# Linear attention stage: scores in row groups of 32, values in column groups by head pair, squares summed with the mask stationary

## The chip, the cores and the metric

One Trainium2 chip, one of its cores. The metric is the device time of one launch in microseconds (us), lower is better. The core has TensorE (PE: matmuls; PEld is its weight load), VectorE (DVE), ScalarE (ACT), GpSimd (POOL) and SyncE (SP, which issues the DMAs). Each engine works through its own instruction list in order, and waits for the others by semaphores.

## The reference

The kernel computes five residual layers on x (32 sequences of 32 tokens, 256 features). Only one of them, `L1_attn`, is touched. It works on chunks of 16 tokens with a carried matrix W; since the score mask and the carried state together are linear, the kernel computes it as causal attention without softmax over each sequence:

```python
q = l2norm(silu(short_conv(h @ Wq.T, conv_q)).reshape(b, l, 16, 16))   # k likewise, v without l2norm
inter = einsum('bqhk,bhkv->bqhv', q_c, W)            # W starts as W_init
qk    = einsum('bqhd,bkhd->bhqk', q_c, k_c) * tril
intra = einsum('bhqk,bkhv->bqhv', qk, v_c)
W_new = W + einsum('bchk,bchv->bhkv', k_c, v_c)
o = layernorm_per_head(inter + intra) * ln_gamma + ln_beta
out = (o * (h @ Wg.T)) @ Wo.T
```

There are 16 heads of 16 features, so 8 heads lie on 128 partitions, and everything is fp32.

## The kernel before

The program is six stages (cross attention, a selective scan, attention with experts, an alignment by dynamic programming, this linear attention, and a last expert layer), each written as one function per engine: `t_load`, `t_pe`, `t_act`, `t_dve`, `t_pool` here. There is no scheduler: the order of the Python lines is the order on each engine, and every wait is written out. Activations lie with features on partitions, as two groups c of 128, and 1024 tokens along the free axis, in 8 tiles t of 128 tokens (4 sequences each).

The stage in order:

1. Layer norm (`norm_pe`, `norm_act`, `norm_dve`). Then `dense_pe` (L201) makes 16 groups of 128x512: q, k, v and the gate (n = 0 to 3). ACT copies each to SBUF (L2025).
2. DVE runs the short convolution of q, k, v, six halves in a row, four instructions each (L2077, L2080). ACT applies Silu in place (L2030) and squares q and k (L2034); it does so only after all 16 copies.
3. PE sums the squares of each head (L1948): 32 matmuls in which a 128x128 block of squares is the stationary operand and the head mask (8 columns) streams. ACT takes the root (L2037), DVE the reciprocal (L2087) and spreads it over the 16 features (L2088). PE turns v (L1957) and the spread norms (L1967), DVE multiplies q and k by them (L2093, eight instructions).
4. The tile loop. POOL builds q times the head mask, so that eight heads stand side by side (L2160, two of 128x1024 a tile). `sc(t)` multiplies k by it (L1978, four matmuls of 512 columns into PSUM banks 0 to 3), DVE masks the four banks (L2100), and PE adds, in bank 4 or 5, q times W_init (L1989) and for each head its scores (128x128, stationary) times 16 columns of v (L1994), 16 matmuls a tile. ACT evicts the tile (L2047).
5. The per-head layer norm in two halves (`centre`, `variance`, `scaled`), the turn back (L2002), the gate (L2136), the output projection (L2010) and the residual add (L2152). `centre(0)` stands in the tile loop ahead of the last mask, `variance(0)` and `scaled(0)` behind it. The next stage starts at the small MEMSET on L174.

An fp32 matmul shows in the trace as two records, each with a weight load of its own; a transpose as one.

Of the kernel before, what the change touches and what calls it, by code (L numbers as in the profile page):

```python
# [13 lines left out]
ALU = mybir.AluOpType  # L14
# [50 lines left out]
         + [(3, "tile_qblk", "d_ms", TT), (3, "tile_norm", "d_tm", TT), (3, "tile_rec", "d_add", TT)]  # L65
# [64 lines left out]
def build(nc, A, out, first=0, last=5):  # L130
    ctx = ExitStack()
    with ctx:
# [1784 lines left out]
        t_qm = [view(26 * K + 2048 * j, DC, HPC, P) for j in range(2)]  # L1917
        t_S = [view(30 * K + 2048 * j, XH, P) for j in range(2)]
# [5 lines left out]
        t_ns = view(38 * K, 2, 2 * P)  # L1924
# [11 lines left out]
        def t_pe(pe):  # L1936
            norm_pe(pe, "tn", xT, U[2])
            pe.wait_ge(*S.at("tn_out", 2))
            pe.wait_ge(*S.at("ld_t", dma_n["ld_t"]))
            dense_pe(pe, "tp", [(P, [(t_w[n][:, k, m * P:(m + 1) * P], half(U[1], k, h)) for k in range(DC)])  # L1940
                                for n in range(4) for m in range(DC) for h in range(NH)], "a" * 16, list(range(8)))

            pe.wait_ge(*S.at("tp_ev_a", 16))
# [6 lines left out]
            mm.then_inc(S["t_ss"], 1)  # L1950
            pe.wait_ge(*S.at("t_root", 1))
            pe.wait_ge(*S.at("t_silu", 6))
            for t in range(TT):
                for c in range(DC):
                    o = (t % 2) * D + c * P

                    mm = nc.tensor.transpose(ps[:, 4 + (t // 2 + 1) % 4, o:o + P], t_x[2][:, c, t * P:(t + 1) * P], ident)  # L1957
                if t % 2:
                    mm.then_inc(S["t_vT"], 1)

            pe.wait_ge(*S.at("t_rn", 1))
            for g in range(8):
                n, c, h = g // 4, (g // 2) % 2, g % 2
                if g >= 4:
                    pe.wait_ge(*S.at("t_qk", g - 3))
                for t in range(4 * h, 4 * h + 4):
                    mm = nc.tensor.transpose(ps[:, g % 4, (t % 4) * P:(t % 4 + 1) * P],  # L1967
                                             t_rep[:, n, t, c * P:(c + 1) * P], ident)
# [4 lines left out]
            def sc(t):  # L1973
                for b in range(4):
                    if t:
                        pe.wait_ge(*S.at("t_mask", 4 * (t - 1) + b + 1))
                    pe.wait_ge(*S.at("t_qm", 2 * t + b // 2 + 1))
                    nc.tensor.matmul(ps[:, b, :], t_x[1][:, b // 2, t * P:(t + 1) * P],  # L1978
                                     t_qm[t % 2][:, b // 2, 4 * (b % 2):4 * (b % 2) + 4, :].rearrange("p h q -> p (h q)"),
                                     start=True, stop=True).then_inc(S["t_s"], 1)  # L1980

            sc(0)
            for t in range(TT):
                if t + 1 < TT:
                    sc(t + 1)
                if t >= 2:
                    pe.wait_ge(*S.at("t_oev", t - 1))
                for c in range(DC):
                    nc.tensor.matmul(ps[:, 4 + t % 2, c * P:(c + 1) * P], t_x[0][:, c, t * P:(t + 1) * P],  # L1989
                                     t_W0[:, c, :], start=True, stop=False, skip_group_check=True)  # L1990
                    for hd in range(HPC * c, HPC * (c + 1)):
                        if hd % 4 == 0:
                            pe.wait_ge(*S.at("t_mask", 4 * t + hd // 4 + 1))
                        mm = nc.tensor.matmul(ps[:, 4 + t % 2, hd * DK:(hd + 1) * DK], t_S[t % 2][:, hd, :],  # L1994
                                              t_v[:, t, hd * DK:(hd + 1) * DK], start=False,
                                              stop=True, skip_group_check=True)
                mm.then_inc(S["t_om"], 1)
# [18 lines left out]
            turn(1)  # L2016
            project(1)

        def t_act(act):
            norm_act(act, "tn", U[1], U[2], 0)  # L2020
            for g in range(16):
                n, m, h = g // 4, (g // 2) % 2, g % 2
                act.wait_ge(*S.at("tp_mm", g + 1))
                dst = (t_raw + [t_g])[n]
                nc.scalar.copy(half(dst, m, h), ps[:, g % 8, :]).then_inc(S["tp_ev_a"], 1)  # L2025
# [5 lines left out]
            for n in range(4):  # L2031
                silu(n)
                act.wait_ge(*S.at("t_silu", n + 1))
                nc.scalar.activation(t_sq[n // 2][:, n % 2, :], t_x[n // 2][:, n % 2, :],  # L2034
                                     ACT.Square).then_inc(S["t_sq"], 1)
            act.wait_ge(*S.at("t_ss", 1))
            nc.scalar.activation(t_ns[:, 0, :], ps[:, 4, 0:2 * P], ACT.Sqrt, bias=eps[:, 3:4]).then_inc(S["t_root"], 1)  # L2037
            silu(4)
            silu(5)
            for n in range(4):  # L2040
                act.wait_ge(*S.at("t_vT", n + 1))
                nc.scalar.copy(t_v[:, 2 * n:2 * n + 2, :].rearrange("p a b -> p (a b)"), ps[:, 4 + (n + 1) % 4, :])\
                    .then_inc(S["t_vev"], 1)

            def evict(t):
                act.wait_ge(*S.at("t_om", t + 1))
# [11 lines left out]
            for t in range(TT - 2):  # L2058
                evict(t)
            squares(0)  # L2060
            evict(TT - 2)
# [5 lines left out]
        def t_dve(ch):  # L2067
# [3 lines left out]
            dve.wait_ge(*S.at("ld_t", dma_n["ld_t"]))  # L2071
            for n in range(6):
# [6 lines left out]
                for s in range(1, KW):  # L2079
# [6 lines left out]
            dve.wait_ge(*S.at("t_root", 1))  # L2086
            ln(v.reciprocal(t_ns[:, 1, :], t_ns[:, 0, :]))  # L2087
            v.tensor_copy(t_rep.rearrange("p n t (h d) -> p (n t h) d", d=DK),  # L2088
                          t_ns[:, 1, :].unsqueeze(2).broadcast_to([P, 2 * P, DK])).then_inc(S["t_rn"], 1)
            for g in range(8):  # L2090
                x = half(t_x[g // 4], (g // 2) % 2, g % 2)
                dve.wait_ge(*S.at("t_nrm", g + 1))
                v.tensor_tensor(x, x, ps[:, g % 4, :], ALU.mult).then_inc(S["t_qk"], 1)  # L2093

            def masked(t):
                if t >= 2:
                    dve.wait_ge(*S.at("t_om", t - 1))
                for b in range(4):
                    dve.wait_ge(*S.at("t_s", 4 * t + b + 1))
                    v.tensor_tensor(t_S[t % 2][:, 4 * b:4 * b + 4, :],  # L2100
                                    ps[:, b, :].rearrange("p (h q) -> p h q", h=4),
                                    t_tril.unsqueeze(1).broadcast_to([P, 4, P]), ALU.mult).then_inc(S["t_mask"], 1)


# [28 lines left out]
            def gated(h):  # L2133
                dve.wait_ge(*S.at("t_oT", h + 1))
                for c in range(DC):
                    v.tensor_tensor(half(t_x[0], c, h), ps[:, 2 * c + h, :], half(t_g, c, h),  # L2136
                                    ALU.mult).then_inc(S["t_gate"], 1)
            for t in range(TT - 1):
                masked(t)
            centre(0)  # L2140
            masked(TT - 1)
            variance(0)
            scaled(0)
# [10 lines left out]
        def t_pool(pool):  # L2154
            pool.wait_ge(*S.at("t_qk", 4))
            for t in range(TT):
                for c in range(DC):
                    if t >= 2:
                        pool.wait_ge(*S.at("t_s", 4 * (t - 2) + 2 * c + 2))
                    nc.gpsimd.tensor_tensor(t_qm[t % 2][:, c],  # L2160
                                            t_x[0][:, c, t * P:(t + 1) * P].unsqueeze(1).broadcast_to([P, HPC, P]),
                                            hmask.unsqueeze(2).broadcast_to([P, HPC, P]),
                                            ALU.mult).then_inc(S["t_qm"], 1)
# [316 lines left out]
```

## Time and profile before

| | |
|---|---|
| time, median of 3 runs | 1930.89 us (1924.90 to 1931.84) |
| the profiled execution's own time | 1929.83 us |
| its span | 1928.2 us |
| busy, share of the span | PE 87%, DVE 55%, ACT 39%, POOL 39%, weight load 42% |
| this stage, from the layer norm's first matmul to the next stage's start | 1508.15 to 1666.24 us |

Busy times are of one profiled execution. PE's records are modelled at their ends, so that a stretch full of records is not PE at its peak. The granted clock (PEclk) is a share of 2.4 GHz; TensorE runs at 2.4 or at 1.2 GHz, and 0.89 is a mean over stretches at either.

### The profile page before, as it was taken

To read this page: it belongs to the slowest core of one execution; us is meant where nothing else is said; L and a number is where in the kernel's file an instruction comes from. 1 tells how busy PE (TensorE), PEld (TensorE's weight loads), DVE (VectorE), ACT (ScalarE), POOL (GpSimd) and SP (SyncE) were. 2 spreads that over 40 slices of the span, in tenths; PEclk is the share of its full clock that TensorE was granted. 3 is DMA by queue.
4 is the path that set the end of the run, shared out by engine and by line. 5 is a ranking of instruction groups with operands and counts; after the bars stand their busy time and mean duration, and the time that the engine had idled before them with its cause. 6 is when DMAs were issued, how large, how long until landed. Compare 5 with 4: busy or idle time off the path is not lost.

```text
span 1928.2 us, 24024 instructions
## 1 busy us (share of the span) xinstructions
PE 1672.4 (87%) x8816; PEld 806.3 (42%) x8816; DVE 1059.2 (55%) x1548; ACT 755.5 (39%) x1191; POOL 746.0 (39%) x452
## 2 busy tenths in 40 slices
PE   7888886886999999999997769999803979899998
PEld 4666663541222232222224525444401557644443
DVE  2444444465998998998993333222368464422121
ACT  1333332275776776776771222111414240122121
POOL 0433331238998998998993010000000023000000
PEclk8999997788999999999999668999855879699999
DMA  2111101003000100100102400111071100100110
GB/s 68 33 33 33 33 27 53 0 14 104 8 19 7 28 16 8 30 13 8 31 5 67 176 0 1 49 33 33 15 168 39 33 0 1 45 9 35 44 44 22
DMA packets 37895, 66.64 MB, mean 35 GB/s; under 512 B 13764, under 2 KB 24408, under 8 KB 36260
## 3 DMA queue, kind: packets, MB, share of 16 engines
q1 hardware_dynamic: 34612, 64.47, 11.3%
q10 hardware_dynamic: 3200, 1.07, 0.2%
q8 instruction: 51, 0.84, 0.2%
q14 instruction: 32, 0.26, 0.0%
HBM read 56.33 MB, written 9.20 MB: 34 GB/s over the span
## 4 chain that ended last, share of the span: by engine, by line
PE 51%; POOL 22%; DVE 12%; issue 11%; DMA 2%; ACT 2%; SPq 1%; DVEq 0%; ACTq 0%; POOLq 0%
POOL arena L1247 20%; PE ps L1467 6%; PE ps L2203 6%; PE ps L2214 6%; PE ps L201 3%; PE ps L1480 3%; PE ps L342 3%; PE ps L347 3%; PE ps L224 3%; PE ps L360 2%; DVE arena L477 2%; PE ps L1978 2%; PE ps L1994 2%; DVE arena L488 1%; PE ps L217 1%
## 5 line engine op out<-in xcount | busy, mean ns | idle before, releaser
L1247 POOL TENSOR_TENSOR arena<-arena 128x768 f32<-128x768 f32 x248 | 532.4, 2187 | 23.2 <-DVE arena L1164 23.2
L867 PE MATMUL ps<-arena 32*128 32x512 f32 x1520 | 316.7, 653 | 0.9 <-ACT arena L1052 0.9
L1167 DVE TENSOR_TENSOR arena<-arena,ps 128x1024 f32<-128x1024 f32 x248 | 302.1, 1218 | 10.2 <-POOL arena L1247 5.5
L2160 POOL TENSOR_TENSOR arena<-arena 128x1024 f32<-128x1024 f32 x16 | 30.0, 1896 | 433.3 <-DVE arena L2093 418.6
L1045 ACT ACTIVATE arena<-arena 128x1024 f32<-128x1024 f32 x124 | 131.1, 1057 | 136.3 <-DVE arena L1147 136.3
L1147 DVE TENSOR_TENSOR arena<-arena,ps 128x1024 f32<-128x1024 f32 x124 | 151.4, 1221 | 22.0 <-PE ps L878 9.5
L915 PE MATMUL ps<-arena 128*32 128x512 f32 (+15 forms) x1024 | 136.9, 607 | 10.4 <-DVE arena L1167 9.9
L1052 ACT ACTIVATE arena<-ps 128x1024 f32<-128x1024 f32 x124 | 127.0, 1024 | 24.8 <-PE ps L867 9.7
L1054 ACT ACTIVATE arena<-arena 128x1024 f32<-128x1024 f32 x124 | 131.1, 1057 | 3.9
L1467 PE MATMUL ps<-arena 128*128 128x512 f32 x288 | 131.9, 602 | 0.5 <-ACT arena L1532 0.5
L867 PEld LDWEIGHTS ps<-arena 32*128 32x128 f32 x1520 | 103.3, 186 | 65.3 <-issue 58.6
L2295 DVE TENSOR_TENSOR arena<-arena,ps 128x512 f32<-128x512 f32 x56 | 38.5, 688 | 159.0 <-ACT arena L2257 159.0
L2203 PE MATMUL ps<-arena 128*128 128x512 f32 x256 | 117.4, 603 | 0.0
L2214 PE MATMUL ps<-arena 128*128 128x512 f32 x256 | 114.1, 600 | 0.0
L887 PE MATMUL ps<-arena 64*128 64x512 bf16 x744 | 104.4, 387 | 0.0
L2257 ACT ACTIVATE arena<-ps,arena 128x512 f32<-128x512 f32 x56 | 38.5, 687 | 162.8 <-PE ps L2203 162.8
L1587 DVE TENSOR_TENSOR arena<-arena,ps 128x512 f32<-128x512 f32 x36 | 24.8, 688 | 128.2 <-PE ps L1467 126.7
L201 PE MATMUL ps<-arena 128*128 128x512 f32 x168 | 81.8, 648 | 9.7 <-DVE arena L269 3.9
L1467 PEld LDWEIGHTS ps<-arena 128*128 128x128 f32 x288 | 55.5, 194 | 68.4 <-issue 66.5
L1532 ACT ACTIVATE arena<-ps 128x512 f32<-128x512 f32 x36 | 21.5, 597 | 157.8 <-PE ps L1467 157.8
L1155 DVE TENSOR_TENSOR arena<-arena 128x256 f32<-128x256 f32 x124 | 82.1, 662 | 0.0
L2214 PEld LDWEIGHTS ps<-arena 128*128 128x128 f32 x256 | 49.1, 192 | 62.6 <-issue 61.9
(306 smaller groups left out, 2400.6 us busy)
## 6 DMA issues: line engine op xcount, KB each, us to landing
arena<-ctxT SPq DMA_DIRECT2D x32, 257.0 KB, 3.0
arena<-ctxT SPq DMA_DIRECT2D x8, 1028.0 KB, 15.7
arena<-L_ffn_w SPq DMA_DIRECT2D x16, 512.0 KB, 4.3
arena<-ctx_rows SPq DMA_DIRECT2D x8, 960.0 KB
arena<-L_ffn_eW SPq DMA_DIRECT2D x8, 512.0 KB, 3.7
m_rows<-arena SPq DMA_DIRECT2D x12, 256.0 KB, 2.8
arena<-m_rows SPq DMA_DIRECT2D x32, 64.0 KB
m_yd<-arena SPq DMA_DIRECT2D x64, 32.0 KB, 2.3
```

Of the source, the lines that this page charges most:

```text
L201: last_mm = nc.tensor.matmul(dst, lhsT, rhs, start=(k == 0), stop=(k == len(pairs) - 1))
L867: mm = nc.tensor.matmul(ps[:, bank + jj, :], weights[r], m_row[r, n // CH % 2, n % CH, :], start=start, stop=True)
L915: mm = nc.tensor.matmul(ps[32 * j:32 * j + rows, 6 + v % 2, :], m_C[:, o - rows:o], m_h[:, u, n % 2, jj, :], start=True, stop=True)
L1045: nc.scalar.activation(m_xa[:, 0, n % 2], m_xa[:, 0, n % 2], ACT.Exp, scale=-1.0).then_inc(S["m_dec"], 1)
L1052: nc.scalar.activation(m_xa[:, 1, n % 2], ps[:, bank:bank + 2, :], ACT.Exp).then_inc(S["m_lus"], 1)
L1054: nc.scalar.activation(m_xa[:, 1, n % 2], m_xa[:, 1, n % 2], ACT.Exp, scale=-1.0).then_inc(S["m_dec"], 1)
L1147: nc.vector.tensor_tensor(m_xa[:, 0, n % 2], m_EA.unsqueeze(1).broadcast_to([P, 2, DI]), ps[:, bank:bank + 2, :], ALU.mult).then_inc(S["m_ ...
L1167: nc.vector.tensor_tensor(m_h[:, u, n % 2], m_xa[:, u, n % 2], ps[:, bank:bank + 2, :], ALU.add).then_inc(S["m_use"], 1)
L1247: nc.gpsimd.tensor_tensor(x, x, m_h[:, u, (n - 1) % 2].rearrange("p j d -> p (j d)")[:, own], ALU.mult).then_inc(S["m_kept"], 1)
L1467: mm = nc.tensor.matmul(ps[:, 4 + part, :], f_w13[j][:, k, part * D + f * P:part * D + (f + 1) * P], half(U[2], k, h), start=(k == 0), sto ...
L2203: mm = nc.tensor.matmul(ps[:, 4 + f % 2, :], g_w1[j][:, k, f * P:(f + 1) * P], half(U[1], k, h), start=(k == 0), stop=(k == 1))
L2214: mm = nc.tensor.matmul(ps[:, 2 * m + h, :], g_w2[j][:, f, m * P:(m + 1) * P], g_h[h][:, f, :], start=False, stop=stop and f == FC - 1, sk ...
```

## The change

Four parts, all in this stage.

- Scores: q is multiplied by two masks instead of eight (`t_par`: the even or the odd head of a pair), so a 32-partition row group holds one head pair. `sc(t)` issues 8 matmuls of 32 rows and 256 columns: four row groups, each to its own bank, for each c. DVE masks two banks by one instruction; POOL makes one of 128x512 a tile.
- Values: v (32 columns, a head pair) is stationary, and the scores of both heads stream (256 columns), into one of four column groups of PSUM partitions. The result has features on partitions and is half waste (the wrong head of the pair): ACT scales the odd part by its mask (`odd`), DVE adds the even part (`pick`), and PE turns the tile to tokens (`by_token`).
- Squares: the head mask, padded to 32 columns by POOL, is stationary, and 512 columns of squares stream, 8 matmuls, with q and k halves in their own column group. The root is now taken on 128x1024, and turned by 8 transposes.
- Order: the four gate groups move from `dense_pe` into the tile loop (t = 1 to 4), their copies too. ACT's first Silu and squares stand between its copies. The multiply by the norms goes by token half, and `sc(0)` waits for the first four of its eight.

```diff
@@ t_pe
             dense_pe(pe, "tp", [(P, [(t_w[n][:, k, m * P:(m + 1) * P], half(U[1], k, h)) for k in range(DC)])
-                                for n in range(4) for m in range(DC) for h in range(NH)], "a" * 16, list(range(8)))
+                                for n in range(3) for m in range(DC) for h in range(NH)], "a" * 12, list(range(8)))
...
             for n in range(4):
                 pe.wait_ge(*S.at("t_sq", n + 1))
-                for t in range(TT):
-                    o = (n // 2) * P + t * XH + (n % 2) * HPC
-                    mm = nc.tensor.matmul(ps[:, 4, o:o + HPC], t_sq[n // 2][:, n % 2, t * P:(t + 1) * P], hmask,
+                for h in range(NH):
+                    mm = nc.tensor.matmul(ps[32 * n:32 * n + 32, 4 + h, :], t_hmask, half(t_sq[n // 2], n % 2, h),
                                           start=True, stop=True)
...
+            def sc(t):
+                pe.wait_ge(*S.at("t_qm", t + 1))
+                for c in range(DC):
+                    for r in range(4):
+                        if t and c == 0 and r % 2 == 0:
+                            pe.wait_ge(*S.at("t_mask", 2 * (t - 1) + r // 2 + 1))
+                        rows = slice(32 * r, 32 * r + 32)
+                        mm = nc.tensor.matmul(ps[:, r, c * D:(c + 1) * D], t_x[1][rows, c, t * P:(t + 1) * P],
+                                              t_qm[t % 2][rows, c].rearrange("p i q -> p (i q)"), start=True, stop=True)
...
+            def weigh(t):
+                if t >= 2:
+                    pe.wait_ge(*S.at("t_oev", t - 1))
+                pe.wait_ge(*S.at("t_mask", 2 * t + 2))
+                for c in range(DC):
+                    cols = slice(c * D, (c + 1) * D)
+                    nc.tensor.matmul(ps[:, 4 + t % 2, cols], t_W0[:, c, :],
+                                     t_x[0][:, c, t * P:(t + 1) * P].unsqueeze(1).broadcast_to([P, 2, P]),
+                                     start=True, stop=False, skip_group_check=True)
+                    for r in range(4):
+                        o = c * P + 32 * r
+                        mm = nc.tensor.matmul(ps[32 * r:32 * r + 32, 4 + t % 2, cols], t_v[:, t, o:o + 32],
+                                              t_S[t % 2][:, r, c, :], start=False, stop=True, skip_group_check=True)
+                mm.then_inc(S["t_om"], 1)
+
+            def by_token(t):
+                pe.wait_ge(*S.at("t_pick", t + 1))
+                for c in range(DC):
+                    mm = nc.tensor.transpose(ps[:, 4 + t % 2, c * P:(c + 1) * P], t_oc[t % 2][:, c, :], ident)
+                mm.then_inc(S["t_tok"], 1)
...
+            sc(0)
             pe.wait_ge(*S.at("t_qk", 8))
...
             for t in range(TT):
                 if t + 1 < TT:
                     sc(t + 1)
...
+                if 1 <= t < 5:
+                    gate(t - 1)
+                weigh(t)
+                if t:
+                    by_token(t - 1)
+            by_token(TT - 1)
@@ t_dve
+                for b in range(2):
+                    dve.wait_ge(*S.at("t_s", 4 * t + 2 * b + 2))
+                    v.tensor_tensor(t_S[t % 2][:, 2 * b:2 * b + 2].rearrange("p r c (i q) -> p (r c i) q", i=2),
+                                    ps[:, 2 * b:2 * b + 2, :].rearrange("p r (h q) -> p (r h) q", h=4),
+                                    t_tril.unsqueeze(1).broadcast_to([P, 8, P]), ALU.mult).then_inc(S["t_mask"], 1)
+
+            def pick(t):
+                dve.wait_ge(*S.at("t_odd", t + 1))
...
             for t in range(TT - 1):
                 masked(t)
+                if t:
+                    pick(t - 1)
             centre(0)
             masked(TT - 1)
+            pick(TT - 2)
             variance(0)
+            pick(TT - 1)
             scaled(0)
```

On PE, in the middle of the tile loop, one tile of the kernel before: L1978 are the scores, L1989 is q times W_init and L1994 the heads' values. The two pieces between 128x128 rows are the two groups c.

```order
L1978 MATMUL ps<-arena 128x512 x4
L1989 MATMUL ps<-arena 128x128
L1994 MATMUL ps<-arena 128x16 x8
L1989 MATMUL ps<-arena 128x128
L1994 MATMUL ps<-arena 128x16 x8
```

The same tile of the changed kernel: L1987 are the scores in row groups, L2018 the gate (in four of the tiles), L1998 is q times W_init, L2003 the values in column groups, L2010 the turn to tokens.

```order
L1987 MATMUL ps<-arena 128x256 x8
L2018 MATMUL ps<-arena 128x512 x2
L1998 MATMUL ps<-arena 128x256
L2003 MATMUL ps<-arena 32x256 x4
L1998 MATMUL ps<-arena 128x256
L2003 MATMUL ps<-arena 32x256 x4
L2010 MATMUL ps<-arena 128x128 x2
```

The 22 matmuls of a tile became 20, or 22 with the gate, and the last two turn the tile before; PE now changes some six times a tile between whole-array and packed matmuls.

On ACT, between the layer norm and the tile loop, the kernel before (L2025 copies a projection, L2030 is Silu, L2034 the square, L2037 the root):

```order
L2025 COPY arena<-ps 128x512 x16
L2030 ACT_TABLE_LOAD
L2030 ACTIVATE arena<-arena 128x1024
L2034 ACTIVATE arena<-arena 128x1024
L2030 ACTIVATE arena<-arena 128x1024
```

The changed kernel, the same place (L2064 copies, L2069 Silu, L2073 square, L2086 root):

```order
L2064 COPY arena<-ps 128x512 x8
L2069 ACT_TABLE_LOAD
L2069 ACTIVATE arena<-arena 128x1024
L2073 ACTIVATE arena<-arena 128x1024
L2064 COPY arena<-ps 128x512 x2
L2069 ACTIVATE arena<-arena 128x1024
L2073 ACTIVATE arena<-arena 128x1024
```

The first squares stand behind 8 copies, not behind 16.

On DVE, at the end of the tile loop, the changed kernel (L2164 masks, L2170 is `pick`, L2185 to L2187 `centre`, L2191 `variance`, L2196 to L2199 `scaled`):

```order
L2185 TENSOR_REDUCE arena<-arena 128x64
L2186 TENSOR_SCALAR arena<-arena 128x64
L2187 TENSOR_TENSOR arena<-arena 128x1024
L2164 TENSOR_TENSOR arena<-ps,arena 128x1024 x2
L2170 SCALAR_TENSOR_TENSOR arena<-ps,arena 128x256
L2191 TENSOR_REDUCE arena<-arena 128x64
L2170 SCALAR_TENSOR_TENSOR arena<-ps,arena 128x256
L2196 RECIPROCAL arena<-arena 128x64
```

The last `pick`, which waits for the last tile's values, now stands ahead of `scaled(0)`.

## Rows read from the trace of the kernel before

**Rows 1.** Busy by stretch: us; engines' busy; granted clock, DMA share, GB/s.
```profile
1528.00:1558.00 30.00, 25.78 (x71) 12.54 (x69) 29.20 (x24) 14.18 (x20) 0.00 (x0) 0.97 0.00 0
1558.00:1570.00 12.00, 10.54 (x50) 10.44 (x49) 0.92 (x1) 6.10 (x7) 0.00 (x0) 0.50 0.00 0
1583.00:1649.00 66.00, 66.00 (x355) 48.81 (x354) 30.32 (x41) 5.56 (x11) 26.55 (x15) 0.89 0.00 1
1649.00:1666.00 17.00, 12.29 (x30) 5.56 (x28) 12.71 (x16) 1.40 (x2) 0.00 (x0) 0.71 0.00 0
```

**Rows 2.** The chain that ended last, in order of time: start us, us, what.
```profile
1555.52 13.04 PE ps L1948 x64
...
1570.36 2.01 ACT arena L2030 x2
1572.51 3.65 PE ps L1957 x16
1576.16 0.85 PE ps L1967 x4
1577.03 4.89 DVE arena L2093 x8
1582.01 7.14 PE ps L1978 x16
```

**Rows 3.** Timeline of DVE before the tile loop: start us, us, engine, line, operation.
```profile
1554.13 3.73 DVE L2080 SCALAR_TENSOR_TENSOR arena<-arena 128x992 f32<-128x992 f32 x3
1569.08 1.75 DVE L2087 RECIPROCAL arena<-arena 128x256 f32<-128x256 f32 x1 [11.23 <-ACT arena L2037]
1570.87 2.29 DVE L2088 COPY arena<-arena 128x4096 f32<-128x4096 f32 x1
```

**Rows 4.** Timeline of PE, one tile of the loop at the full clock.
```profile
1592.93 3.68 PE L1978 MATMUL ps<-arena 128*128 128x512 f32 x8
...
1596.66 1.86 PE L1994 MATMUL ps<-arena 128*128 128x16 f32 x16
...
1600.38 0.86 PE L1978 MATMUL ps<-arena 128*128 128x512 f32 x1
```

**Rows 5.** Groups by line and shape: busy us, mean ns, idle before.
```profile
L2100 DVE TENSOR_TENSOR arena<-ps,arena 128x512 f32<-128x512 f32 x32 | 22.1, 692 | 31.3 <-PE ps L1978 30.9
L2160 POOL TENSOR_TENSOR arena<-arena 128x1024 f32<-128x1024 f32 x16 | 30.0, 1896 | 433.3 <-DVE arena L2093 418.6 <-PE ps L1978 14.7
L2047 ACT COPY arena<-ps 128x256 f32<-128x256 f32 x8 | 3.0, 372 | 66.3 <-PE ps L1994 66.3
L1903 DVE TENSOR_TENSOR arena<-arena,ps 128x256 f32<-128x256 f32 x8 | 3.4, 422 | 12.9 <-PE ps L1729 12.8
L1147 DVE TENSOR_TENSOR arena<-arena,ps 128x1024 f32<-128x1024 f32 x124 | 151.4, 1221 | 22.0 <-PE ps L878 9.5
```

**Rows 6.** Timeline of PE in the scan stage, where matmuls are packed.
```profile
700.67 1.37 PE L867 MATMUL ps<-arena 32*128 32x512 f32 x8
702.04 1.06 PE L915 MATMUL ps<-arena 128*20 128x512 f32 x8
703.03 0.39 PE L878 MATMUL ps<-arena 32*128 32x512 bf16 x2
```

**Rows 7.** Timeline of DVE and ACT at the end of the stage.
```profile
1641.62 1.28 ACT L2056 ACT_TABLE_LOAD   x1
1642.91 0.35 ACT L2056 ACTIVATE arena<-arena 128x64 f32<-128x64 f32 x1
1643.29 0.55 DVE L2128 RECIPROCAL arena<-arena 128x64 f32<-128x64 f32 x1 [4.17 <-ACT arena L2056]
1643.88 1.23 DVE L2129 TENSOR_TENSOR arena<-arena 128x1024 f32<-128x1024 f32 x1
1648.72 1.22 DVE L2117 TENSOR_REDUCE arena<-arena 128x64 f32<-128x1024 f32 x1 [1.10 <-ACT arena L2047]
...
1666.24 0.06 DVE L174 MEMSET arena<- 128x1 f32 x1
```

More of the change, by code:

```diff
@@ L1970, in t_pe @@
             pe.wait_ge(*S.at("t_vev", 4))
-            pe.wait_ge(*S.at("t_qk", 8))
[L1973 to L1980, printed above, removed]
@@ new lines, in by_token, with gate @@
+            def by_token(t):
[3 more added lines that the diff above has]
+                mm.then_inc(S["t_tok"], 1)
+            def gate(g):
+                m, h = g // 2, g % 2
+                if g >= 2:
+                    pe.wait_ge(*S.at("tp_ev_a", 12 + g - 1))
+                for k in range(DC):
+                    mm = nc.tensor.matmul(ps[:, 6 + h, :], t_w[3][:, k, m * P:(m + 1) * P], half(U[1], k, h),
+                                          start=(k == 0), stop=(k == DC - 1))
+                mm.then_inc(S["tp_mm"], 1)
@@ L2016, in t_pe @@
             turn(1)
+            pe.wait_ge(*S.at("tp_ev_a", 16))
             project(1)
@@ L2020, in t_act, with copies @@
             norm_act(act, "tn", U[1], U[2], 0)
[L2021 to L2025, printed above, removed]
+            def copies(lo, hi):
+                for g in range(lo, hi):
+                    n, m, h = g // 4, (g // 2) % 2, g % 2
+                    act.wait_ge(*S.at("tp_mm", g + 1))
+                    dst = (t_raw + [t_g])[n]
+                    bank = g % 8 if n < 3 else 6 + h
+                    nc.scalar.copy(half(dst, m, h), ps[:, bank, :]).then_inc(S["tp_ev_a"], 1)
             def silu(n):
@@ L2030, in silu, with square @@
                 nc.scalar.activation(x, x, ACT.Silu).then_inc(S["t_silu"], 1)
-            for n in range(4):
-                silu(n)
+            def square(n):
                 act.wait_ge(*S.at("t_silu", n + 1))
@@ L2035, in t_act @@
                                      ACT.Square).then_inc(S["t_sq"], 1)
+            copies(0, 8)
+            silu(0)
+            square(0)
+            copies(8, 10)
+            silu(1)
+            square(1)
+            copies(10, 12)
+            for n in (2, 3):
+                silu(n)
+                square(n)
             act.wait_ge(*S.at("t_ss", 1))
-            nc.scalar.activation(t_ns[:, 0, :], ps[:, 4, 0:2 * P], ACT.Sqrt, bias=eps[:, 3:4]).then_inc(S["t_root"], 1)
+            nc.scalar.activation(t_sd2, ps[:, 4:6, :].rearrange("p a b -> p (a b)"), ACT.Sqrt,
+                                 bias=eps[:, 3:4]).then_inc(S["t_root"], 1)
             silu(4)
@@ L2057, in deviation @@
                                      bias=eps[:, 0:1], scale=1.0 / DK).then_inc(S["t_sd"], 1)
-            for t in range(TT - 2):
-                evict(t)
+            for t in range(TT - 1):
+                if 1 <= t < 5:
+                    copies(12 + t - 1, 12 + t)
+                odd(t)
+                if t:
+                    evict(t - 1)
             squares(0)
+            odd(TT - 1)
             evict(TT - 2)
@@ L2071, in t_dve @@
             dve.wait_ge(*S.at("ld_t", dma_n["ld_t"]))
+            ln(v.tensor_reduce(t_par, hmask.rearrange("p (a i) -> p i a", i=2), AX.X, ALU.add))
             for n in range(6):
@@ L2097, in masked @@
                     dve.wait_ge(*S.at("t_om", t - 1))
[L2098 to L2102, printed above, removed]
+                for b in range(2):
[5 more added lines that the diff above has]
+                dve.wait_ge(*S.at("t_odd", t + 1))
+                v.scalar_tensor_tensor(out=t_oc[t % 2], in0=ps[:, 4 + t % 2, :].rearrange("p (c i q) -> p c i q", c=DC, i=2)[:, :, 0, :],
+                                       scalar=t_par[:, 0:1], in1=t_odd[t % 2], op0=ALU.mult, op1=ALU.add).then_inc(S["t_pick"], 1)
             def heads(x, h):
```

89 lines of the change are left out of this document (51 added, 38 removed).

## The prediction

> **What bounds the kernel now.** I read the busy time by stretch first, to see which part of the stage belongs to which engine. Up to 1558 us DVE is full with the convolutions (29.20 of 30 us) at a clock of 0.97; from 1558 to 1570 DVE has almost nothing to do and PE runs at 0.50, the lower of its two levels; from 1583 to 1649 PE has a record in every microsecond and DVE 30 of 66; behind that DVE leads again [rows 1]. Then the chain of waits in order of time: it goes through PE's projections, ACT, the 13.04 us of squares summed on L1948, two Silu on ACT, the turns of v and of the norms, DVE's eight multiplies, and at 1582.01 into the tile loop, where it stays on PE [rows 2]. So the stage has a gap between the last convolution (ends 1554.13 + 3.73 = 1557.86 [rows 3]) and the first mask of the loop, in which a chain of short things runs, and a loop bound by PE. The first mask starts at about 1583.1: the first scores at 1582.01 plus one matmul of 0.86 and some 0.27 until DVE has it (it is a difference of two starts; I use 1583.1). The loop's far end is DVE's first `centre(1)` instruction at 1648.72, and from there it is 17.5 us to the next stage at 1666.24 [rows 7]. The loop is thus 65.6 us.
>
> **Prices.** An fp32 matmul of 512 columns is two records; 16 records took 7.14 us [rows 2], so 0.43 us a record in a stream after the 0.2 us that the last one hangs over, 0.86 us a matmul. Streaming goes by columns, so 256 columns are 0.43 us a matmul. Packed matmuls do run beside each other in this trace: four fp32 matmuls of 512 columns in four column groups took 1.06 us, and four in row groups 1.37 us, where the second pair had waited for a semaphore; one after the other each four would be 3.44 us [rows 6]. So a packed group of four with 256 columns costs 0.43 us. A change between forms: from the first record of L915 to that of L878 are 0.99 us for two rounds of 0.43, so 0.13 us for the change and the first weight load together [rows 6]. I take 0.1 and keep as bounds 0 and 1.06 (the time of a whole packed group, as if it had to be run out once more).
>
> **Part 1, before the loop.** ACT's squares no longer wait for 16 copies. The last half whose squares are needed is the fourth of six. A half takes some 5.0 us on DVE (three of its four instructions are 3.73 [rows 3]), so it is done two halves before 1557.9, at 1547.9; Silu and square add 2.1 (two Silu were 2.01 [rows 2]), 1550.0. The last 2 of the 8 new squares matmuls take 1.7, the root on 128x1024 about 1.0 (a Silu's size; its table load of 1.28 [rows 7] runs beside the matmuls), eight transposes 1.8 (L1957: 3.65 for 16 [rows 2]). That ends near 1555.5, before the last convolution. The 13.04 us of L1948 and 11.23 us of DVE's wait [rows 3] are gone from the path, and what is late next is Silu of the last v half: 1557.9 + 1.1 = 1559.0. Then v's turn 3.65, 1562.7; one group of norm turns 0.85 and 0.3 latency, so the first multiply at 1563.9. DVE meanwhile does the reciprocals from PSUM (1.75 for 256 elements, in two halves, say 1.9) and the spread (2.29): 1557.9 + 4.4 = 1562.3, which just hides. Eight multiplies, 4.89: 1568.8. `sc(0)` needs only the first four and POOL's 0.95 (half of 1896 ns [rows 5]) and fits beside the last four, so the first mask starts at about 1568.9. Gain 1583.1 - 1568.9 = 14.2 us. Bounds: 11 (the padded transposes, reciprocals from PSUM or POOL cost twice what I take) and 17 (PE already at the full clock, which saves half of v's turn and of the rest). The four gate groups leaving `dense_pe` give nothing here, since DVE's convolutions are the cover of both; in the loop they cost.
>
> **Part 2, the loop.** By PE, at the full clock. Scores: two packed rounds of 0.43 plus 0.43 for the pair that waits for the second mask, and two times 0.1: 1.5 us (before 3.68 [rows 4]). Values: two times (0.43 + 0.43), and four changes of form: 2.1 us; before, twice L1994's 1.86 and L1989, so that a tile was 7.45 us from one first score record to the next [rows 4]. The turn: two records, 0.11 each at the full clock (half of L1957's 0.23 at the lower [rows 2]), and a change, 0.4 with some slack. Gate: two matmuls of 0.86 and a change, 1.8, in four tiles. So 4.0 us a plain tile, 5.8 with a gate. DVE: two masks of 1.22 (L1147 reads 128x1024 from PSUM in 1221 ns [rows 5]) and a `pick` of 0.42 (L1903): 2.9 us, less than PE, but scores have one set of banks, so the DVE waits 1.0 us for PE after each mask: 3.8 us, just under PE's 4.0. ACT: 0.37 + 0.37 + 0.59, covered. POOL: 0.95 a tile instead of 3.8, covered.
>
> The sum: first mask 1568.9 to 1571.4. Rest of sc(1) and values of tile 0: 3.0, 1574.4. Four gate tiles, 23.2, 1597.6. Tiles 5 and 6, 8.0, 1605.6. The last mask is late, because `centre(0)` (2.7 us: 1.2 + 0.2 + 1.2) stands before it on DVE: it ends at 1607.6, and the last values at 1609.8. `odd` and `pick` of tile 7 end at 1611.0. Behind this `pick` stands `scaled(0)`; its deviation on ACT is behind the eviction of tile 6 and a table load of 1.28 + 0.35 [rows 7], so it starts at 1612.6 and takes 4.3 (0.55 and three of 1.23 [rows 7]): `centre(1)` starts at 1616.9. In the kernel before `scaled(0)` was hidden by PE's last tiles; now it is on the path. The clock was 0.89 over the loop [rows 1]; with some of the new loop at the lower level too, PE's 35 us grow by 10%, 3.5 us: 1620.4. The loop is 51.5 us instead of 65.6, a gain of 14.1.
>
> The Trainium skill speaks against a part of this: TensorE: Matmul & The Clock Gate, Part 3, says that weight loads overlap running matmuls only if their row group differs. The values' column groups share all rows. By the page 16 loads a tile, 128 in all, would be exposed, and at the 0.1 us that I allow for a change and its load the sum would rise by 13 us, to about 1914. The trace does not agree: four such matmuls, eight records, took 1.06 us with all their loads [rows 6], so the sum leaves it out.
>
> **Part 3, behind it.** The tail of 17.5 us has the same instructions. Total 14.2 + 14.1 = 28.3 us from the profiled execution's 1929.83: 1901.5 us. The median of runs shown is 1930.89, 1.1 above, which is within their scatter.
>
> **Rivals.** (a) The clock stays at the lower level in the loop. For it: PE had 0.50 in 1558 to 1570 with records in 10.5 of 12 us, all with 8 columns, and 0.71 in the tail [rows 1]; the new loop has more waits and short transposes. Against: the packed scan stage ran its records at full speed (0.43 a record [rows 6]). Doubling PE's terms (8.0 and 11.6 us a tile) ends the loop at 1647.4: the loop gains 1.3 and the clock also takes part of the 14.2, so 1917 to 1928. Half the loop so: 1915.
>
> The skill's same page, Part 4, says that transposes do not count as activity for the clock. The new loop has two in 20 or 22 matmuls, so the rule bears on one in ten of its matmuls, and no row here tells the two kinds apart.
>
> (b) The packed matmuls of this stage run one after another: scores 8 x 0.43, values 10 x 0.43, turn and changes 1.0: 8.7 us a tile, 70 us and 7 of gates against 65.6; with 14.2 gained and 2 lost behind the last tile, 1929. Against: [rows 6]. This is also the case that the change does not do what it says.
>
> (c) Slower: each change of form drains the array and costs 1.06 us instead of 0.1. Six a tile, 48 in the loop, all on PE's path: 46 us, 1948. The forecast's gain is used up at 0.69 us each, and slower by over 0.5% begins at 0.89. The rows show 0.1 between forms, but none between whole-array and packed fp32.
>
> The Trainium skill, TensorEngine Tiling (Array Packing), Tiling Modes, states that changing the mode drains TensorE; it gives no price. The 0.13 from L915 to L878 [rows 6], from column groups to row groups, is such a change.
>
> (d) Faster: scores' two rounds overlap fully, `scaled(0)` finds room before the last `pick`, and PE is at full speed: 3.5 + 4 + 3 us more, 1891.
>
> **Numbers.** The forecast has 0.66, (d) 0.10, (a) 0.14, (b) 0.04, (c) 0.06. Its own range is 1894 to 1911. With (a) and (d) the range is 1888 to 1922. Half a per cent, 9.7 us, is what a measurement can tell. Faster holds the forecast, (d) and most of (a): 0.87; same is the rest of (a) and (b): 0.07; slower 0.06.
>
> **What would show it.** The first mask near 1569; no wait of DVE for the root over 1 us; the eight score matmuls within 1.5 us; a value group of four in about 0.5 us behind its W_init matmul; gate tiles 1.8 us longer than plain ones; DVE, not PE, last before the second `centre`; the clock of the loop near 0.89. It is wrong if the value matmuls start one after another, if score records start 0.2 us apart within a round, or if the clock of the loop is under 0.7.

## The result, and the profile after

The changed kernel takes 1900.61 us (median of 4 runs, 1898.74 to 1902.01); the kernel before, run beside it, 1931.19 (4 runs). The ratio is 0.9848, 95% interval 0.9826 to 0.9871: 1.5% faster, 30.6 us. The forecast was 1901.5, 28.3 us below the profiled execution of before.

The profiled execution took 1902.01 us, its span is 1900.4. The stage runs from 1511.23 to 1638.44 us: 127.2 us instead of 158.2, so 31.0 us were won in it. It begins 3.2 us later than in the profile of before, though nothing ahead of it was changed; everything behind it takes the same 262.0 us. Where I compare parts below, I therefore take distances between two starts in the same stage.

VectorE's timeline of the changed kernel from the last convolution to the second tile's mask (columns as in [rows 3]; L2149 is the reciprocal, L2152 the spread, L2157 multiplies, L2164 masks):

```profile
1557.28 3.73 DVE L2141 SCALAR_TENSOR_TENSOR arena<-arena 128x992 f32<-128x992 f32 x3
1560.92 1.94 DVE L2149 RECIPROCAL arena<-ps 128x128 f32<-128x128 f32 x2
1562.89 2.36 DVE L2152 COPY arena<-arena 128x2048 f32<-128x2048 f32 x2
1566.46 4.87 DVE L2157 TENSOR_TENSOR arena<-arena,ps 128x512 f32<-128x512 f32 x8 [1.20 <-PE ps L1974]
1571.25 2.34 DVE L2164 TENSOR_TENSOR arena<-ps,arena 128x1024 f32<-128x1024 f32 x2
1574.98 2.35 DVE L2164 TENSOR_TENSOR arena<-ps,arena 128x1024 f32<-128x1024 f32 x2 [1.39 <-PE ps L1987]
```

The wait of 11.23 us before the reciprocal [rows 3] is gone. From the end of the convolutions (1561.01) to the first mask are 10.2 us, 25.3 before.

PE's timeline ahead of the loop (L1953 squares, L1959 the root turned, L1965 v, L1974 norms, L1987 scores), to be read against [rows 2]:

```profile
1547.54 2.24 PE L1953 MATMUL ps<-arena 128*32 128x512 f32 x8
1550.88 1.90 PE L1953 MATMUL ps<-arena 128*32 128x512 f32 x4 [1.10 <-ACT arena L2073]
1553.32 1.90 PE L1953 MATMUL ps<-arena 128*32 128x512 f32 x4 [0.53 <-ACT arena L2073]
1556.52 1.06 PE L1959 MATMUL ps<-arena 128*128 128x128 f32 x8 [1.30 <-ACT arena L2086]
1562.15 3.67 PE L1965 MATMUL ps<-arena 128*128 128x128 f32 x16 [4.56 <-ACT arena L2069]
1565.61 4.10 PE L1974 MATMUL ps<-arena 128*128 128x128 f32 x32
1569.64 1.15 PE L1987 MATMUL ps<-arena 32*128 32x256 f32 x16
```

The turned root is ready (1557.58) over 3 us before DVE can take it (1560.92). One more thing shows: the first two squares groups take 2.24 us for 8 records, less than one after the other (4 x 0.86): they stand in different column groups and run beside each other.

PE in one gate tile of the loop (L2018 the gate, L1998 q times W_init, L2003 values, L2010 turn) and in a plain one, to be read against [rows 4]:

```profile
1585.42 1.15 PE L1987 MATMUL ps<-arena 32*128 32x256 f32 x16
1586.50 1.98 PE L2018 MATMUL ps<-arena 128*128 128x512 f32 x4
1588.32 0.59 PE L1998 MATMUL ps<-arena 128*128 128x256 f32 x2
1588.84 0.64 PE L2003 MATMUL ps<-arena 128*32 128x256 f32 x8
1588.84 0.16 PEld L2003 LDWEIGHTS ps<-arena 128*32 128x32 f32 x8 [0.33 <-issue]
1589.41 0.70 PE L1998 MATMUL ps<-arena 128*128 128x256 f32 x2
1590.04 0.64 PE L2003 MATMUL ps<-arena 128*32 128x256 f32 x8
1590.61 0.44 PE L2010 MATMUL ps<-arena 128*128 128x128 f32 x2
1590.98 1.15 PE L1987 MATMUL ps<-arena 32*128 32x256 f32 x16
...
1602.10 1.15 PE L1987 MATMUL ps<-arena 32*128 32x256 f32 x16
1603.17 0.70 PE L1998 MATMUL ps<-arena 128*128 128x256 f32 x2
...
1605.93 1.15 PE L1987 MATMUL ps<-arena 32*128 32x256 f32 x16
```

A gate tile is 5.56 us, a plain one 3.84, before 7.45 [rows 4]. All eight score matmuls (16 records) take 1.08 us, a value group of four (8 records) 0.57 with the change to the next form. The start of the loop is slower: the second tile's scores and the first tile's values took 3.12 and 4.20 us (1.08 and 2.3 later on), the scores in part because they waited for the first tile's masks. The busy time by stretch (columns of [rows 1]) has the reason. The rows are the end of the work ahead of the loop, the loop's start, the rest of it up to PE's last matmul, and the whole loop. The clock was largely at its lower level at the start, and at the upper one from there to PE's last matmul. Over the whole loop its mean is 0.89, the same as over the loop of before, 1583.14 to 1648.72.

```profile
1561.00:1571.20 10.20, 8.64 (x64) 7.78 (x64) 8.93 (x13) 3.40 (x5) 2.26 (x3) 0.75 0.00 0
1571.20:1580.00 8.80, 7.38 (x40) 3.08 (x44) 4.75 (x5) 0.00 (x0) 1.85 (x2) 0.61 0.01 2
1579.86:1615.72 35.86, 33.23 (x272) 15.35 (x268) 21.49 (x24) 9.65 (x21) 4.16 (x4) 1.00 0.00 1
1571.25:1620.91 49.66, 40.47 (x304) 18.29 (x304) 30.34 (x34) 10.81 (x23) 5.96 (x6) 0.89 0.00 1
```

The loop's end on DVE (L2170 `pick`, L2196 the start of `scaled`, the second L2185 that of `centre(1)`), to be read against [rows 7]:

```profile
1609.23 2.35 DVE L2164 TENSOR_TENSOR arena<-ps,arena 128x1024 f32<-128x1024 f32 x2
1611.49 0.47 DVE L2170 SCALAR_TENSOR_TENSOR arena<-ps,arena 128x256 f32<-128x256 f32 x1
1611.89 1.21 DVE L2191 TENSOR_REDUCE arena<-arena 128x64 f32<-128x1024 f32 x1
1614.74 0.48 DVE L2170 SCALAR_TENSOR_TENSOR arena<-ps,arena 128x256 f32<-128x256 f32 x1 [1.64 <-ACT arena L2097]
1616.66 0.55 DVE L2196 RECIPROCAL arena<-arena 128x64 f32<-128x64 f32 x1 [1.44 <-ACT arena L2111]
...
1620.91 1.21 DVE L2185 TENSOR_REDUCE arena<-arena 128x64 f32<-128x1024 f32 x1
```

### The profile page after: what moved, and what is told of

It reads as the page before. It is cut to its first block, busy times and chain, and to the rows that moved or that the text cites. A ratio compares the mean times of both kernels' runs of the same rounds, so it can differ in the third digit from the quotient of the medians.

```text
span 1900.4 us, 23822 instructions
## 1 busy us (share of the span) xinstructions
PE 1637.5 (86%) x8711; PEld 761.8 (40%) x8728; DVE 1059.2 (56%) x1543; ACT 758.9 (40%) x1199; POOL 724.5 (38%) x446
## 3 DMA queue, kind: packets, MB, share of 16 engines
q1 hardware_dynamic: 34612, 64.47, 11.5%
## 4 chain that ended last, share of the span: by engine, by line
PE 48%; POOL 22%; DVE 14%; issue 12%; DMA 2%; ACT 2%; SPq 1%; DVEq 0%; ACTq 0%; POOLq 0%
POOL arena L1249 20%; PE ps L1469 6%; PE ps L2279 6%; PE ps L2290 6%; PE ps L1482 3%; PE ps L344 3%; PE ps L349 3%; PE ps L226 2%; PE ps L203 2%; PE ps L362 2%; DVE arena L479 2%; DVE arena L2141 1%; DVE arena L490 1%; PE ps L219 1%; PE ps L869 1%
## 5 line engine op out<-in xcount | busy, mean ns | idle before, releaser
L1469 PEld LDWEIGHTS ps<-arena 128*128 128x128 f32 x288 | 55.5, 194 | 68.4 <-issue 66.7
L1722 PE MATMUL ps<-arena 96*86 96x96 bf16 x34 | 9.7, 287 | 76.1 <-DVE arena L1891 75.9
```

The lines of the kernel that those rows point to most:

```text
L1469: mm = nc.tensor.matmul(ps[:, 4 + part, :], f_w13[j][:, k, part * D + f * P:part * D + (f + 1) * P], half(U[2], k, h), start=(k == 0), sto ...
```

## The experiments

Every kernel below is the changed kernel with one or two edits. The table holds, from each one's profiled execution, DVE's starts: convolutions' end to the first multiply by the norms, the multiplies to the first mask, the first mask to `centre(1)` (the loop), and `centre(1)` to the next stage; all in us. The times are medians of all runs; each ratio is to runs of the kernel before made beside that kernel (medians 1930.43 to 1931.19 us). The stretch ahead of the convolutions was 20.0 or 21.6 us in these profiles, whatever the kernel, and is left out. Where the stage begins also moved, from 1506.0 to 1516.7 us, though no edit touches anything ahead of it; so a time can differ by more than the stage does.

| kernel | to the multiplies | to the first mask | loop | tail | time |
|---|---|---|---|---|---|
| before | 19.2 | 6.1 | 65.6 | 17.5 | 1931.19 |
| changed | 5.5 | 4.8 | 49.7 | 17.5 | 1900.61 |
| e1_old_loop | 5.5 | 4.8 | 78.3 | 17.0 | 1926.11 |
| e2_values_unpacked | 5.7 | 4.8 | 64.9 | 17.0 | 1914.44 |
| e6_squares_old | 6.2 | 4.8 | 49.8 | 17.7 | 1900.03 |
| e7_act_old | 7.8 | 5.2 | 52.2 | 17.0 | 1901.06 |
| e8_both_old | 12.2 | 4.8 | 49.9 | 17.0 | 1906.72 |
| e3_gate_idle | 4.2 | 4.8 | 44.6 | 17.4 | 1891.17 |
| e4_gate_dense | 4.8 | 5.1 | 43.2 | 17.0 | 1892.85 |
| e5_filler | 4.8 | 5.1 | 50.0 | 16.9 | 1898.08 |
| e9_tail | 5.6 | 4.8 | 46.6 | 17.5 | 1895.59 |
| e10_gate_tail | 4.2 | 4.8 | 41.3 | 17.3 | 1888.47 |
| e11_gate_hole_tail | 4.2 | 4.8 | 38.3 | 17.6 | 1888.28 |

**The old loop.**

```diff
-    mm = nc.tensor.matmul(ps[:, r, c * D:(c + 1) * D], t_x[1][rows, c, t * P:(t + 1) * P], ...)   # and weigh, pick, by_token
+    nc.tensor.matmul(ps[:, b, :], t_x[1][:, b // 2, t * P:(t + 1) * P], ...)                      # as before the change
```

> The changed kernel with scores, masks, queries and values of the tile loop as before the change (eight heads by mask, 16 value matmuls a tile); squares, ACT's order and the place of the gate stay new. My account: the loop goes back to PE's pace, 7.45 us a tile plus 1.8 in four gate tiles, so first mask to the second centre takes 65.6 + 7.3 = 73 us instead of 49.7, and the time is 1900.6 + 23 = about 1924 us. Rival, the gain came from the work ahead of the loop and packing gives little: under 1908 us.

1926.11 us, ratio to before 0.9987 (0.9971 to 1.0003). Packing is worth 25.5 us here, my account, and the rival is out: without it, what was won ahead of the loop is spent on the gate and the clock inside it. The loop is 78.3 us, 5 more than the 73 expected. The clock was 0.84 over it, and 0.89 over the same form of loop before [rows 1]. At 0.84 some 25 of 78.3 us are at the lower level, at 0.89 some 14 of 65.6; half of the difference, 5 to 6 us, is an estimate of what it cost, and it fits. Why this loop lost more clock than that of before, with the same 16-column matmuls and the gate's long ones added, stays open.

```profile
1569.35:1647.66 78.31, 77.94 (x367) 53.45 (x366) 29.96 (x42) 7.90 (x15) 26.49 (x15) 0.84 0.00 1
```

**The values alone.**

```diff
-    mm = nc.tensor.matmul(ps[32 * r:32 * r + 32, 4 + t % 2, cols], t_v[:, t, o:o + 32], t_S[t % 2][:, r, c, :], ...)
+    mm = nc.tensor.matmul(ps[:, 4 + t % 2, hd * DK:(hd + 1) * DK], t_S[t % 2][:, r, c, i * P:(i + 1) * P],
+                          t_v[:, t, hd * DK:(hd + 1) * DK], ...)     # 16 a tile; odd, pick and by_token left out
```

> The changed kernel with only the values unpacked: scores in row groups stay, but each head's scores are stationary again and 16 columns of v stream (16 matmuls a tile), and the odd part, the pick and the turn to tokens fall away. My account: values were 3.9 us a tile in that form and are 2.3 plus 0.4 for the turn now, so 8 x 1.2 = 10 us more, less 2 us at the end of the loop, where scaled(0) is no longer behind the last pick: about 1908.5 us. Rival, the three extra steps a tile eat what the column groups give: 1900.6 within 2 us, or below it.

1914.44 us, ratio 0.9924 (0.9895 to 0.9952): the rival is out, and the value groups are worth 14 us, not the 8 of my account. PE's timeline shows why: a tile of values takes 4.0 us at the upper level and 7.7 at the lower, and not only tile 0 (the first row) but the last two as well ran at the lower one.

```profile
1576.76 3.43 PE L2001 MATMUL ps<-arena 128*128 128x16 f32 x16
...
1602.33 0.39 PE L1997 MATMUL ps<-arena 128*128 128x128 f32 x2
1602.55 1.86 PE L2001 MATMUL ps<-arena 128*128 128x16 f32 x16
...
1628.41 0.78 PE L1997 MATMUL ps<-arena 128*128 128x128 f32 x2
1628.98 3.43 PE L2001 MATMUL ps<-arena 128*128 128x16 f32 x16
```

The granted clock over the last two tiles' values, with the last tile's scores:

```profile
1618.70:1636.00 17.30, 17.30 (x89) 16.50 (x89) 8.51 (x8) 3.43 (x5) 0.00 (x0) 0.50 0.00 1
```

PE shows as busy in all 17.3 us of it, 64 of the 89 records being value matmuls of 16 columns, and had the lower level. Tiles of the same form between 1587.4 and 1618 us ran at the upper one, so the form alone doesn't settle it.

**Squares, and ACT's order.** The first edit is the old sum, the second the old order, the third both.

```diff
-    mm = nc.tensor.matmul(ps[32 * n:32 * n + 32, 4 + h, :], t_hmask, half(t_sq[n // 2], n % 2, h), ...)
+    mm = nc.tensor.matmul(ps[:, 4, o:o + HPC], t_sq[n // 2][:, n % 2, t * P:(t + 1) * P], hmask, ...)   # 32 of them
```
```diff
-    copies(0, 8); silu(0); square(0); copies(8, 10); silu(1); square(1); copies(10, 12)
+    copies(0, 12); silu(0); square(0); silu(1); square(1)
```

> The changed kernel with only the sum of squares in its old form (32 matmuls with the squares stationary and 8 columns streaming, root on 128x256, no turn). My account: with squares spread between the copies, only the last 8 of these matmuls come behind the last square, some 3 to 5 us, which end near the last convolution, so the form of this sum is hidden by DVE's convolutions: 1900.6 within 1 us. Rival, the 13 us of the old sum are what the new form took away: 1909 to 1914 us.

> The changed kernel with only ACT's order as before (12 copies, then all Silus and squares); the new sum of squares stays. My account: the last square ends some 4 us later, and the root, its turn and the last Silu with it, so the turn of v and the first mask are about 2 us late: stage 129, time 1902.5 us. With the run that undid both (stage 133.6) and the one that undid the form alone (129.9) this tells whether the two parts add up or stand in for each other. Rival: 6 us or more, if ACT's order alone carries what the two gave together.

> The changed kernel with the sum of squares in its old form and ACT's order as before (all 12 copies, then Silu and squares). My account: now the squares come late and their 13 us of matmuls stand behind them; the last Silu, which waits behind the root on ACT, is about 6.6 us later than in the changed kernel: 1907 us, where the old form alone costs nothing. Rival, either of the two carries the gain by itself and they add up: then this run is the sum of the two single undoings.

The old sum alone: 1900.03 us (ratio 0.9842, 0.9816 to 0.9868), no change; 0.7 us later at the multiplies. The old order alone: 2.3 us later at the multiplies as expected, 1901.06 (0.9846, 0.9831 to 0.9861), which a time can't tell from the changed kernel's. (Its profiled execution was the longest of its four, 1904.27 us; the 2.5 us by which its loop is longer lie in the last tile, whose values ran at the lower clock in it, 4.3 us instead of 2.4.) Both: 6.7 us later, 1906.72 (0.9886, 0.9858 to 0.9915), 6.1 us slower than the changed kernel. They don't add up and don't quite stand in for each other: 0.7 + 2.3 is under half of 6.7. In the profile of e8 all 64 records of the sum come behind ACT's late squares and take 12.88 us, as in [rows 2], and end 3.7 us behind the convolutions; with either part new they are done before the convolutions end. So the title's third part, the squares' form, gives nothing beside the new order; with the old order it is worth 5.7 us (1906.72 against 1901.06).

```profile
1546.65 12.88 PE L1954 MATMUL ps<-arena 128*128 128x8 f32 x64 [4.23 <-ACT arena L2071]
```

There is a third repair of the same lateness, which e8 leaves in place. Its multiplies start 12.2 us behind the convolutions, those of the kernel before 19.2. With 12 copies ahead of it and not 16, ACT's first Silu came 11.5 us ahead of the convolutions' end, and 4.6 us ahead of it in the kernel before. So with the old form and the old order the gate's leaving the projections seems worth some 7 us (read from these two profiles; no run makes this edit alone); with both new it is worth nothing, as e4 below shows. The other 1.3 us, from the multiplies to the first mask (6.1 before, 4.8 to 5.2 in every run), fit `sc(0)` starting beside the second half of the multiplies; no run takes that part out.

**Where the gate stands.**

```diff
+    if n == 1: gate(0)          # behind the second half's squares; gate(1) behind the last, gate(2), gate(3) behind the turned root
-    if 1 <= t < 5: gate(t - 1)  # in the loop
```

> The changed kernel with the four gate groups taken out of the tile loop and put where PE waits ahead of it: one behind the second half's sum of squares, one behind the last, two behind the turn of the root. Their copies go between ACT's Silus. My account: the loop loses 4 x 1.8 = 7.2 us, PE idles over 7 us there so nothing is added but 0.6 us of waiting for the last copies, and with PE busy up to the turn of v the clock is at its upper level for it and for the first two tiles (3.7 to 2.2 us, and some 3 us in tiles 0 and 1): 1900.6 - 7.2 + 0.6 - 4 = 1890 us. Rival 1, the loop is not bound by PE once the gate is gone (DVE's masks): gain of 4 us or less, 1897. Rival 2, the matmuls push the root's turn late and give back what the loop gains: 1900.

> The changed kernel with the four gate groups back in the projections, where they were before the change. My account: the loop loses 7.2 us; the projections end 6.9 us later, so all eight sums of squares run behind them, the root and its turn come some 5 us later and the reciprocals with them, first mask about 3 us later; the clock helps the turn of v: about 1900.6 - 7.2 + 3 - 1.5 = 1895 us. Rival, moving the gate into the loop was what freed the work ahead of it, and undoing it costs as much as it gives: 1900 or more.

e3: 1891.17 us (ratio 0.9784, 0.9768 to 0.9800), e4 with all 16 groups in the projections: 1892.85 (0.9800, 0.9782 to 0.9819). They are 9.4 and 7.8 us faster than the changed kernel and not told apart by time. The profiled execution of e3 was the longest of its six, 1901.00 us (the others 1888.67 to 1893.74), but its stage is 6.4 us shorter than the changed kernel's: it begins 5.4 us later. In both the loop falls by 5 to 6.5 us, towards the 7.2 of four gates, since tiles at 3.84 us are still PE's, and both rivals are out. Neither was late with the root: with the other parts in place, moving the gate into the loop freed nothing ahead of it. My account of e3 had the clock up for the first tiles; in its profile it is at the lower level from 3.2 to 10.0 us behind the first mask.

**Clock or gate.**

```diff
+    for _ in range(5): nc.tensor.matmul(ps[:, 0, 0:D], ident, xT[:, 0, 0:D], start=True, stop=True)   # behind the turned root
```

> The changed kernel with five matmuls (128x128 stationary, 256 columns of fp32, result thrown away) in the 4.6 us that PE waits for the last Silu. It separates the clock from the gate. My account: they take up to 4.3 us at the lower clock and fit; the clock is up for the turn of v (3.7 to 2.2 us), the norm turns and tiles 0 and 1 (a value part of 4.3 us instead of 2.3 in tile 0): 4 us less, 1896.5. Rival, the clock of the first tiles does not depend on that stretch, since the norm turns stand between: 1900.6 within 1 us.

1898.08 us (0.9825, 0.9811 to 0.9838). The turn of v took 2.77 us instead of 3.67, and the multiplies start 0.7 us earlier, the first mask 0.4; the loop is 50.0. So the rival holds for the loop: its first tiles are slow with that stretch filled, too. The time is 2.5 us lower, but the whole stage is only 0.6 us shorter; the rest lies outside it, where no edit was made, and I can't assign it to the filler.

**The loop's end.**

```diff
 ACT:  squares(0)
+      deviation(0)                 # was behind evict(TT - 2)
       odd(TT - 1); evict(TT - 2)
 DVE:  masked(TT - 1)
-      pick(TT - 2); variance(0); pick(TT - 1); scaled(0)
+      variance(0); pick(TT - 2); scaled(0)     # pick(TT - 1) behind its first multiply
```

> The changed kernel with another order at the loop's end: ACT takes the first half's deviation ahead of the last tile's odd part, DVE the variance ahead of the pick of tile 6, and the last pick stands inside scaled(0), behind its first multiply. My account: scaled(0) starts at 1613.5 instead of 1616.7 and includes one pick of 0.5, so the second centre starts 2.5 us earlier: 1898. Rival, the second centre waits for the last tile's eviction, not for scaled(0): no change, 1900.6.

1895.59 us (0.9821, 0.9804 to 0.9838), 5.0 us faster than the changed kernel, of which the stage accounts for 2.9; the loop is 3.1 us shorter (2.5 expected). `scaled(0)` was on the path, as the forecast said.

**Together, and the hole behind sc(0).**

```diff
     sc(0)
+    pe.wait_ge(*S.at("t_qk", 6))
+    gate(3)                        # e11 only; bank 5, and weigh(1) waits for its copy
     pe.wait_ge(*S.at("t_qk", 8))
```

> The gate groups ahead of the loop, in PE's waits, and the new order at the loop's end, together. Alone they took 6.4 and 2.9 us from the stage. My account: they lie in different places and add up, stage 127.2 - 9.3 = 117.9, time about 1888 us. Rival, without the gate the end of the loop is bound by the last tile's values and turn, and the tail's order gives under 1 us: 1890.5.

> As the run before, but the gate groups stand elsewhere: one behind the second half's sum of squares, two behind the turn of the root, and the last between sc(0) and sc(1), where PE waited 1.8 us for the first mask in every version. My account: the root's turn is not pushed, the hole is filled at no cost, and with a matmul in it the clock stays at its upper level in tiles 0 and 1, which cost 2 to 3 us at the lower: stage 117.9 - 2.5 = 115.4, time 1885.5. Rival, the clock falls there anyway, from what stood ahead of sc(0): 1888 within 1 us, or 1 us above it, since the group may end late.

e10: 1888.47 us (0.9780, 0.9764 to 0.9796); the loop is 41.3, 8.4 us less than the changed kernel's; 5.1 (e3) and 3.1 (e9) add up. e11: 1888.28 (0.9775, 0.9761 to 0.9788). Its loop is 3.0 us shorter still, and PE's timeline shows that tile 0's values now run at the upper level:

```profile
1569.63 1.98 PE L1955 MATMUL ps<-arena 128*128 128x512 f32 x4
1571.54 0.70 PE L2000 MATMUL ps<-arena 32*128 32x256 f32 x4
...
1573.62 0.70 PE L2011 MATMUL ps<-arena 128*128 128x256 f32 x2
1574.25 0.64 PE L2016 MATMUL ps<-arena 128*32 128x256 f32 x8
```

The same place of the changed kernel:

```profile
1575.66 1.22 PE L1998 MATMUL ps<-arena 128*128 128x256 f32 x2
1576.81 1.08 PE L2003 MATMUL ps<-arena 128*32 128x256 f32 x8
```

The first 7.84 us of the loop, e10 and then e11 (columns of [rows 1]):

```profile
1566.30:1574.14 7.84, 6.14 (x36) 2.44 (x36) 4.71 (x5) 0.00 (x0) 1.81 (x2) 0.70 0.01 2
1570.16:1578.00 7.84, 7.52 (x66) 3.46 (x64) 5.89 (x7) 1.06 (x2) 2.39 (x3) 1.00 0.01 2
```

So with one group of matmuls in the 1.8 us hole behind `sc(0)` the clock stays up, and the expectation held for the loop. e11 also moves one other group, from ahead of the root to behind its turn, which no run takes apart from this. But the profiles agree: in all ten kernels that leave a hole of 1.7 to 1.8 us there (the changed one, e2 to e10) the clock falls 1.6 to 3.2 us behind the first mask; in e11 it doesn't, nor in e1, whose longer scores leave no such hole. In the time the two are the same within their scatter (1884.6 to 1892.1 and 1885.1 to 1889.5): 3 us inside a stage are hard to see in 5 runs. Both beat the kernel before by 2.2% and the changed one by 0.6%.

## Why the prediction was right

It was right in size (30.6 us, forecast 28.3) and in its main steps. In the profiles the part ahead of the loop gave 15.1 us (forecast 14.2) and the loop 15.9 (forecast 14.1). The terms, against what they measured:

- Convolutions' end to first mask: forecast 11.0 us, measured 10.2. The next late thing was, as forecast, Silu of the last v half and v's turn (3.67 for 3.65). The root came before DVE needed it. What was not in the forecast: ACT's order, the squares' form and the gate's leaving repair one lateness between them, and with the first in place the form gives nothing (e6). Two small sums of it were off, neither on the path: the turned root's terms add up to 1554.5 and not 1555.5, and DVE's 1.9 and 2.29 to 4.2 and not 4.4.
- Loop: forecast 51.5, measured 49.7. Scores 1.5 forecast, 1.08 measured: I had let one pair wait for the second mask, but in the steady state both masks are done before PE comes to `sc`, by 1.9 us in a gate tile and 0.2 in a plain one. Values 2.1 forecast, 2.29 measured: 0.57 above four streams of 0.43, so a change of form, with the first weight loads behind it, is 0.14 and not 0.1. Tiles 5.8 and 4.0 forecast, 5.56 and 3.84 measured. The clock: I had spread 3.5 us over the loop; it fell only around tile 0 (values 4.2 instead of 2.3) and was at the upper level in the rest of PE's work. Keeping it up there gave 3.0 us (e11), so the size came out near, but by luck: I had taken the 0.89 of the loop of before, and had no reason for where it falls.
- The end: `scaled(0)` on the path, forecast; the order that takes it off gave 3.1 us of loop.
- Tail: unchanged, 17.5 us, forecast and measured.
- What the sum said of the gate, nothing ahead and 7.2 us in the loop, held in the main: a gate tile is 1.7 us longer than a plain one, and taking the gate out gave 5.1 to 6.5 us of loop.

Rival (a) needed half the loop or all of it at the lower level; it was 6.8 us of the loop's start and 3.7 at its end, behind PE's last matmul, and the loops with 16-column values, e1 and e2, were the ones to lose more clock (0.84 and 0.75 over the loop). Rival (b) is refuted by 16 score records in 1.08 us. Rival (c) asked for 0.89 us a change of form and the rows give 0.14. Of rival (d) nothing came true: the scores' two rounds ran one after the other (1.08 us, and one round streams for 0.43), `scaled(0)` was on the path, and the clock fell at the start. The rule of TensorE: Matmul & The Clock Gate, Part 3 (the Trainium skill), by which the value groups would expose their weight loads, is not borne out: eight records with eight loads took 0.57 us, of which 0.43 are streams, and the last of the eight loads ended 0.16 us behind the group's start, beside the first round's streams (the PEld row above).

## What to carry to other kernels

When a stage waits at a clean boundary (here the end of the convolutions), find the first thing behind it that can't be earlier, and count everything else only up to there: repairs of the same lateness don't add up, and once one is made another can be worth nothing. Work that was moved into a loop bound by its engine costs most of its time there (5.1 to 6.5 of 7.2 us); put it into the waits of the engine ahead of the loop, even one of 1.8 us, where it can also keep the clock up. Many small matmuls can cost twice: by their own overhead, and by a clock that can be at its lower level although the engine shows busy all the time.

## What the runs showed of the hardware

- TensorE busy for 17.3 of 17.3 us and yet at the lower level, 0.50, when most of its matmuls had 16 columns (e2); and at the upper one, 1.00, in a loop of packed matmuls with PE busy 33.2 of 35.9 us.
- The clock rose with nothing but transposes on TensorE: PE waited 4.56 us, then ran v's 16 transposes in 3.67 us (0.23 each) and the next 32 in 4.10 (0.13 each). The Trainium skill, TensorE: Matmul & The Clock Gate, Part 4, says that transposes don't count as activity; these rows of the changed kernel (columns of [rows 1]) disagree.

```profile
1562.15:1566.00 3.85, 3.85 (x18) 3.85 (x19) 3.07 (x3) 1.90 (x4) 0.00 (x0) 0.50 0.00 0
1566.10:1569.60 3.50, 3.50 (x31) 3.10 (x29) 3.14 (x6) 0.34 (x1) 1.78 (x2) 1.00 0.00 0
```

- Scores of two rounds and four row groups, each group to its own bank, ran at 16 records in 1.08 us, 0.43 x 2 plus 0.22.
- The stretch ahead of the convolutions was 20.0 or 21.6 us in profiles of the same code, so one profile can't price an edit of 2 us by its end; distances inside a stage can.
